# Layer 2's expert routing: every fourth tile of tokens compared by ScalarE instead of VectorE

## The reference: what is computed

```
probs = softmax(tokens @ router_w.T)
top1_idx, top1_prob = argmax(probs), max(probs)
order = lexsort((-top1_prob, top1_idx))          # by expert, then by falling probability
pos_in_group = place of each token within its expert's part of that order
keep = pos_in_group < capacity                   # capacity = ceil(T / 8 * 1.25)
final_e = where(keep, top1_idx, 0)
out = y of expert final_e, per token
```

## Time and profile before

| | us |
|---|---|
| median of 3 runs | 3621.76 |
| lowest and highest of the 3 | 3619.23, 3622.51 |
| the profiled execution's own time | 3641.51 |
| its span, first to last instruction | 3639.8 |
| busy in the span: PE | 2681.1 |
| DVE | 2130.4 |
| ACT | 1424.6 |
| POOL | 958.4 |

### The profile page before, as it was taken

How to read it: one execution, slowest core, us unless ns; L and a number is a source line. 1 busy time by engine, 2 the same in 40 slices (tenths; PEclk the granted TensorE clock), 3 DMA queues, 4 the chain that set the end, 5 groups by cost and what they waited for, 6 DMA issues and landing times. The chain is left out here.

```text
span 3639.8 us, 31419 instructions
## 1 busy us (share of the span) xinstructions
PE 2681.1 (74%) x8904; PEld 1456.0 (40%) x8904; DVE 2130.4 (59%) x3703; ACT 1424.6 (39%) x3934; POOL 958.4 (26%) x625
## 2 busy tenths in 40 slices
PE   2007888999999979999877776685678787387317
PEld 1003434555555544444344452243344443266203
DVE  7997541322222266666544449214999996678687
ACT  1004433211111146666543321242799898233003
POOL 0003565000000000000122220321899999000005
PEclk7558999999999989999978879897887787699558
DMA  2002112000000065545300030112000000000001
GB/s 51 0 0 47 47 47 64 0 0 0 0 0 0 0 140 144 147 138 146 93 1 0 1 68 5 33 55 80 1 1 1 1 1 1 23 1 1 2 0 30
DMA packets 105950, 124.45 MB, mean 34 GB/s; under 512 B 21628, under 2 KB 59261, under 8 KB 105549
## 3 DMA queue, kind: packets, MB, share of 16 engines
q1 hardware_dynamic: 103660, 118.40, 12.5%
q0 software_dynamic: 2144, 4.41, 0.4%
HBM read 108.57 MB, written 14.19 MB: 34 GB/s over the span
## 5 line engine op out<-in xcount | busy, mean ns | idle before, releaser
L2355 POOL TENSOR_TENSOR dots_pr<-dots_g 128x1536 f32<-128x1536 f32 (+3 forms) x118 | 356.6, 3062 | 73.1 <-DVE dots_g L2480 60.7
L1012 DVE SCALAR_TENSOR_TENSOR attn_sim<-attn_sc,attn_mask 128x512 f32<-128x512 f32 (+3 forms) x256 | 125.9, 492 | 316.9 <-PE attn_sc L938 313.8
L938 PE MATMUL attn_sc<-attn_q,attn_xb 128*128 128x512 f32 (+3 forms) x768 | 295.0, 486 | 0.0
L949 PE MATMUL attn_op<-attn_sim,attn_v 128*128 128x512 f32 (+3 forms) x768 | 295.0, 486 | 0.0
L1298 DVE TENSOR_TENSOR grp_h<-grp_sq,grp_cb 128x512 f32<-128x512 f32 x256 | 176.5, 692 | 191.8 <-ACT grp_sq L1186 171.8
L1126 PE MATMUL grp_po<-grp_h,grp_down 128*128 128x512 f32 x512 | 266.4, 602 | 5.8 <-DVE grp_h L1298 5.7
L2368 PE MATMUL dots_pu<-delta_wE,all_xt 128*128 128x264 f32 x512 | 194.6, 527 | 95.5 <-DVE dots_g L2480 94.1
L1118 PE MATMUL grp_ph<-all_xt,grp_up 128*128 128x512 f32 x512 | 263.8, 598 | 0.5 <-ACT grp_sg L1202 0.5
L1180 ACT ACTIVATE grp_r<-grp_ph 128x512 f32<-128x512 f32 x272 | 162.4, 597 | 185.5 <-PE grp_ph L1118 183.8
L626 POOL TENSOR_TENSOR mix_h<-mix_r,mix_cb 128x512 f32<-128x512 f32 x128 | 179.8, 1416 | 123.8 <-ACT mix_r L540 109.6
L2422 ACT ACTIVATE dots_pr<-dots_pr 128x128 f32<-128x128 f32 x704 | 206.3, 301 | 3.5 <-POOL dots_pr L2355 3.5
(11 more groups left out here) (617 smaller groups left out, 5356.9 us busy)
## 6 DMA issues: line engine op xcount, KB each, us to landing
grp_cb<-grp_combine SPq DMA_DIRECT2D x512, 128.0 KB, 3.1
mix_cb<-top_weights SPq DMA_DIRECT2D x64, 256.0 KB, 3.2
cap_xs<-cap_zero SPq DMA_DIRECT2D x1, 2257.5 KB, 16.7
experts_xe<-cap_xs SPq DMA_DIRECT2D x7, 322.5 KB, 3.4
all_x<-in_L_attn_x_dram SPq DMA_DIRECT2D x4, 512.0 KB, 5.0
cap_w<-in_L_ffn_W_dram SPq DMA_DIRECT2D x1, 2048.0 KB
cap_y<-experts_yo SPq DMA_DIRECT2D x8, 256.0 KB, 2.3
all_xn<-cap_y SPq DMA_DIRECT2D x8, 256.0 KB, 5.1
```

Of the source, the lines that this page charges most:

```text
L938: nc.tensor.matmul(sc[k % SC][:, 0:w], xb[:, m * P:(m + 1) * P], q[:, par, n0:n0 + w], start=True, stop=True).then_inc(s_mm, 1)
L949: ins = nc.tensor.matmul(op[half][:, n0 - half * GROUP:n0 - half * GROUP + w], v[:, par, m], sim[:, par, k, 0:w], start=False, stop=False)
L2355: nc.gpsimd.tensor_tensor(dst, a, key, ALU.mult).then_inc(pp_ready, 1)
```

## The change

Tiles 1, 5, 9, ... 29 (every fourth, 8 of 32) are compared on ACT, all but their own 128 columns. Their results stand in a buffer of their own, `ahead_act`, also two deep. For such a tile ACT first writes `sign` of (own probability - other probability) for all 4096 columns, then turns it into ones and zeros: left of the tile by relu (1 only where the sign is 1), right of it by a sigmoid of 200*sign + 100 (1 where the sign is 0 or 1). The tile's own 128 columns stay on DVE. PE waits for both (`act_ready`, `diag_ready`). The other 24 tiles are compared on DVE as before, two buffers in turn among themselves. The room for the new buffers comes from `cnt`, which now lies in `pb`.

```diff
-        cnt = s.sb("cnt", [E, T])
+        cnt = pb[0:E, :]
+        ahead_act = s.sb("ahead_act", [P, 2, T], BF16)
+        sign = s.sb("sign", [P, T], BF16)
+        steep = s.sb("steep", [P, 1])
+        ON_ACT = [i for i in range(NT) if i % 4 == 1]
+        ON_DVE = [i for i in range(NT) if i not in ON_ACT]
+        def ahead_of(i):
+            return ahead_act[:, ON_ACT.index(i) % 2] if i in ON_ACT else ahead[:, ON_DVE.index(i) % 2]
+        def wait_free(eng, i, mine):
+            k = mine.index(i)
+            if k >= 2:
+                eng.wait_ge(cnt_mm, mine[k - 2] + 1)
...
 PE, for each tile i:
-                    pe.wait_ge(ahead_ready, i + 1)
+                    if i in ON_ACT:
+                        pe.wait_ge(act_ready, ON_ACT.index(i) + 1)
+                        pe.wait_ge(diag_ready, ON_ACT.index(i) + 1)
+                    else:
+                        pe.wait_ge(ahead_ready, ON_DVE.index(i) + 1)
...
 ACT, after the copies of pb:
+                act.wait_ge(steep_made, 1)
+                act.wait_ge(pb_ready, NG)
+                for n, i in enumerate(ON_ACT):
+                    a, b = i * P, (i + 1) * P
+                    if n:
+                        act.wait_ge(act_ready, n)
+                    wait_free(act, i, ON_ACT)
+                    nc.scalar.activation(sign[:], pb[:], ACT.Sign, bias=prob[:, i], scale=-1.0).then_inc(sign_ready, 1)
+                    act.wait_ge(sign_ready, n + 1)
+                    ins = nc.scalar.activation(ahead_of(i)[:, 0:a], sign[:, 0:a], ACT.Relu)
+                    if b < T:
+                        ins = nc.scalar.activation(ahead_of(i)[:, b:], sign[:, b:], ACT.Sigmoid, bias=steep[:], scale=200.0)
+                    ins.then_inc(act_ready, 1)
...
 DVE:
-                    if i >= 2:
-                        dve.wait_ge(cnt_mm, i - 1)
+                    if i in ON_ACT:
+                        wait_free(dve, i, ON_ACT)
+                        stt(to[:, a:b], pb[:, a:b], p_i, before[:], ALU.subtract, ALU.is_lt).then_inc(diag_ready, 1)
+                        continue
+                    wait_free(dve, i, ON_DVE)
```

More of the change, by code:

```diff
@@ L1850, in capacity_route @@
         ahead = s.sb("ahead", [P, 2, T], BF16)
-        cnt = s.sb("cnt", [E, T])
+        cnt = pb[0:E, :]
[4 more added lines that the diff above has]
+        ON_DVE = [i for i in range(NT) if i not in ON_ACT]
+        act_ready, diag_ready, steep_made, sign_ready = (s.sem(n) for n in ("act_ready", "diag_ready", "steep_made", "sign_ready"))
+        def ahead_of(i):
[4 more added lines that the diff above has]
+                eng.wait_ge(cnt_mm, mine[k - 2] + 1)
         number = s.sb("number", [P, NT], mybir.dt.int32)
@@ L1869, in _ @@
             def _(pool):
+                nc.gpsimd.memset(steep[:], 100.0).then_inc(steep_made, 1)
                 nc.gpsimd.memset(before[:], LEAST).then_inc(made, 1)
@@ L1903, in _ @@
                 for i in range(NT):
-                    pe.wait_ge(ahead_ready, i + 1)
+                    if i in ON_ACT:
[3 more added lines that the diff above has]
+                        pe.wait_ge(ahead_ready, ON_DVE.index(i) + 1)
                     for k in range(NG):
-                        ins = nc.tensor.matmul(bank[k][0:E, :], hot16[:, i], ahead[:, i % 2, k * GROUP:(k + 1) * GROUP],
+                        ins = nc.tensor.matmul(bank[k][0:E, :], hot16[:, i], ahead_of(i)[:, k * GROUP:(k + 1) * GROUP],
                                                start=(i == 0), stop=(i == NT - 1))
@@ L1955, in _ @@
                 for i in range(NT):
-                    if i >= 2:
-                        dve.wait_ge(cnt_mm, i - 1)
-                    a, b, p_i = i * P, (i + 1) * P, prob[:, i]
+                    a, b, p_i, to = i * P, (i + 1) * P, prob[:, i], ahead_of(i)
+                    if i in ON_ACT:
[3 more added lines that the diff above has]
+                    wait_free(dve, i, ON_DVE)
                     if i:
-                        ts(ahead[:, i % 2, 0:a], pb[:, 0:a], p_i, None, ALU.is_lt)
+                        ts(to[:, 0:a], pb[:, 0:a], p_i, None, ALU.is_lt)
                     if i < NT - 1:
-                        ts(ahead[:, i % 2, b:], pb[:, b:], p_i, None, ALU.is_le)
-                    stt(ahead[:, i % 2, a:b], pb[:, a:b], p_i, before[:], ALU.subtract, ALU.is_lt).then_inc(ahead_ready, 1)
-                    dve.wait_ge(ahead_ready, i + 1)
+                        ts(to[:, b:], pb[:, b:], p_i, None, ALU.is_le)
+                    stt(to[:, a:b], pb[:, a:b], p_i, before[:], ALU.subtract, ALU.is_lt).then_inc(ahead_ready, 1)
+                    dve.wait_ge(ahead_ready, ON_DVE.index(i) + 1)
                 dve.wait_ge(cntT_mm, 1)
```

## The result

| | before | changed |
|---|---|---|
| median of 6 runs each, us | 3621.84 | 3606.45 |
| lowest and highest | 3619.23, 3622.69 | 3603.39, 3610.25 |
| ratio of changed to before | | 0.996, 95% interval 0.9947 to 0.9972 |
| the profiled execution's own time | 3641.51 | 3609.19 |
| its span | 3639.8 | 3607.5 |

The median became 15.4 us shorter; 17.5 were forecast (3604.3, range 3599.5 to 3609.5). The interval reaches from 10 to 19 us and holds the forecast. How much of the difference to it is real could not be read from this; the traces say more.

The account below looks back on a forecast made before the run. VectorE was taken to set the routing loop's pace before and after. Terms: -21.7 + 3.0 + (2.2 - 1.1) of waits = -17.5 us, so 3621.8 becomes 3604.3; likely range 3600 to 3608, eight in ten 3599.5 to 3609.5.

Parts of the forecast that it names:

- The bound: Routing's comparison loop: VectorE sets the pace, 2.713 us a tile before and 2.13 after; TensorE and ScalarE have room.
- VectorE's price: Comparison loop: eight tiles of 2.713 us go, 21.7 us; their own-column instructions stay at 0.38 each, 3.0 us back.
- The waits at the start: VectorE waits for TensorE to free buffers early in the loop: 0.7 and 1.45 us, 2.2 instead of 1.1 in all.
- ScalarE's price: ScalarE in the loop: 7.5 us a tile, sign 3.71 of it, and one table load of 1.28 us.
- TensorE's waits for VectorE: In the routing's loop, TensorE's waits for VectorE were to fall from 30.9 to about 12 us.
- Behind the loop: After the loop: clearing four new semaphores costs at most 0.2 us, taken as 0; the end stays as before.
- The 19.75 us of the profiled execution: Profiled execution's excess over the median: taken as spread over the whole span, with 0.1 us in the loop.
- Rival A: ScalarE sets the loop's pace, as with table changes every tile at 10.1 us: gain 7.0, time 3614.8; chance 0.05.
- Rival B: TensorE stays at 1.2 GHz in the loop: 22.6 us more, time 3644; chance 0.03.
- Rival C: ScalarE's reading of `pb` slows VectorE's comparisons: at 2% the gain is 16.2 us; chance beyond 10% slowing 0.02.
- The total: Whole kernel: 17.5 us shorter, median from 3621.8 to 3604.3 us.

Follow-up runs that it names:

- e5: Changed kernel with every eighth tile on ScalarE (4 tiles) instead of every fourth; 3641.56 us beside 3650.87 of before, VectorE's loop 79.0 us.
- e7: Changed kernel with three buffers instead of two for VectorE's tiles; 3629.54 us beside 3650.87 of before, VectorE's loop 66.9 us.
- e1: The kernel before, unchanged, profiled a second time; 3634.17 us beside other runs of before with a median of 3628.96.
- e8: Changed kernel with a one-column square root ahead of every sign, so ScalarE's tables change twice a tile; 3644.63 us against 3650.87 of before, ratio 0.9981.
- e9: Changed kernel with a 4096-column copy on ScalarE ahead of its first sign, making tile 1 late; 3609.19 us beside 3626.97, loop 74.1 us.
- e6: Changed kernel with fifteen tiles on ScalarE instead of eight; 3679.22 us against 3650.87 of before, ratio 1.0076.

## Why the prediction was right

**The bound.** VectorE set the pace before and sets it after; the waits say so, and e5 shows that the gain goes by the tiles taken off it. Right.

**VectorE's price.** 8 x 2.713 = 21.7 us were to go, 3.0 to stay. The instruction that stays costs 0.27 us and not 0.38: the 0.38 of the earlier trace rows includes VectorE's wait for its own result, and behind this instruction no such wait stands. I had the lower value, 0.30, in the text and took the higher. That is the mis-sized term: 8 x 0.11 = 0.9 us more gain. Less 0.15 for 2.35 us of waits instead of 2.2, it explains 18.3 of the 18.4 us that the loop gained.

**The waits at the start.** 0.7 and 1.45 us were worked out, 0.85 and 1.50 measured, at the two tiles named. e7 shows that a third buffer takes them away.

**ScalarE's price.** Sign 3.71 us as forecast, tile 7.47 for 7.5, one load of 1.28; tile 1 was ready 5.50 us after VectorE's start (2208.94 against 2203.44), 5.43 forecast. The longest row that the slope came from had half the columns, and the slope held.

**TensorE's waits for VectorE.** "Down from 30.9 to about 12" was forecast, and 15.1 us came, 6.8 of them ahead of the first tile. The forecast gives no working for its 12, so where the 3 us went can't be said. No time hangs on it, since VectorE sets the pace.

**Behind the loop.** The four semaphores cost at most 0.1 us: 1.10 from the end of the last instruction to the first weight load, 1.07 before. The transposes' 0.5 us (3.08 for 3.58) were not forecast: this is a small piece of luck with the clock.

**The 19.75 us of the profiled execution.** This step was wrong. I took them for an addition spread over the span. The first profile holds one stall of 23 us in the experts' stage that e1 and the changed kernel's profile don't have, and the changed kernel's profiled execution was only 2.7 us above its median. So the stall is most likely what they were, though e1, without it, was still 5.2 us above the runs beside it. It did no harm, because the loop's share was taken as nearly nothing, but the sentence was an assumption: that stage's wait of 21.9 us for "remote" stood in the trace of before.

**Rival A.** Not here: one load. e8 made it real, with 10.25 us a tile for 10.1 reckoned. Its gain, 7.0 by the prediction, was 5.5 in the routing and 6.2 by the medians; the difference is mostly the 0.15 us a tile, 1.2 in all, of which the square root is the cause. The drain that the Trainium skill's page "ScalarE: Activation LUTs", section "What ACT_TABLE_LOAD costs", adds to a load did not show at any of the 16 loads of e8; with it e8 would have been slower than before. Its section "Table sets: the hidden batching unit" says that relu and other cheap functions stand in every set; here sign and relu ran both ahead of the sigmoid's load and behind it without another, while a square root made every tile pay for two.

**Rival B.** TensorE kept 2.4 GHz. But the margin was small: tile 1 was ready at 2208.94, TensorE free at 2209.50, 0.6 us. e9 shows what a late tile 1 does, at a price of 4.9 us; with that the kernel is still faster than before. In e6, with a gap in every pair of tiles, the clock did not hold: 0.83 on average. In e8 the gap was 0.65 us, and the clock rose all the same while tile 1 ran.

**Rival C.** The comparisons of 3968 columns, 2287 ns at most before and 2286 in the changed kernel, don't test it, for ScalarE reads `pb` during a small part of the first and not at all during the last. But fifteen others ran wholly or nearly so beside a sign, the one of 3584 columns above among them: 18.71 us together, and 18.73 for the same shapes before. Nothing was lost.

**The total.** 17.5 us were forecast. The medians of the two comparisons gave 15.4 and 16.2 (by the ratios 14.5 and 19.6), the traces 18.8, and the kernel with the time put back came out 0.8 us from before. I hold 18.8 for the effect, 18.4 of it the loop's; the two intervals of the time, 10 to 19 and 15 to 24, agree with it and with the forecast alike. That the first measurement lay 2.1 us beside the forecast says little, since other stages vary by more.

## What to carry to other kernels

When the busiest engine of a loop is given help by an idle one, divide the work by the measured time of a whole unit on each (here 2.71 and 7.47 us): the helper pays only while its unit fits into what the others do meanwhile, and e6 shows the loss on the other side. Then look at the two ends of the loop: at the start, whether the helper's first unit is ready while TensorE's clock is still low, and whether the buffers bridge those slow units; at the end, how many units are left for TensorE when both are done. Where a change is worth 0.5%, read its worth from the length of its stage in the trace, which repeated to 0.1 us here while the whole run's time moved by several; and see at which clock its parts ran, which moved this one by up to 0.8 us.

## What the runs showed of the hardware

- A load of ScalarE's tables took 1.28 us in each of 16 cases (e8). It began at most 0.02 us behind the instruction before it (0.07 for the first), and the one after it began at most 0.02 us later.
- ScalarE and VectorE read the same 128x4096 tile at the same time without slowing each other: 3.71 us for the sign, 2.08 us for VectorE's 3584 columns beside it and 2.08 alone.
- TensorE, idle for 2.9 us at 1.2 GHz, rose to 2.4 GHz only 5.3 us after it began again (e9, one run); with gaps of 2 to 4 us in each 7.47 us it stood at 0.83 on average (e6).
- In 5 of 11 profiles, of four different kernels and before, the experts' stage held waits of 15 to 22 us on ScalarE and VectorE whose releaser is not an engine of the core, and was some 23 us longer. All four kernels measured together as e5 to e8 had it. The cause is open.
